# Gated integers of 30 of 48 units finished inside the up stage of a quantised feed-forward block

## What is computed

```
h    = act_qdq(layernorm(x))
up   = act_qdq(h @ Wup.T);  gate = act_qdq(h @ Wgate.T)
sig  = fixed_qdq_u16(sigmoid(gate))
gate = act_qdq(gate * sig)
o    = act_qdq(gate * up)
out  = x + o @ Wdown.T
```

## Time and profile before

| | |
|---|---|
| median of 3 runs | 2597.03 us (2592.02 to 2599.91) |
| profiled execution | 2596.16 us, its span 2594.1 us |
| gate, up and down stage, PE's matmuls | 751.6 to 1250.7, 1269.0 to 1769.0, 2087.6 to 2587.8 us |
| product stage | 1777.4 to 2062 us |
| PE, DVE, ACT busy over the span | 78%, 75%, 59% |
| DMA | 633.62 MB, mean 244 GB/s |

### The profile page before, as it was taken

The page is one execution under the profiler, slowest core; times in us unless marked ns, Lnnn a source line. Parts: engine busy times, 40 slices in busy tenths (PEclk is TensorE's granted clock), DMA queues, the critical chain, the costliest instruction groups (busy, mean ns, idle before and its releaser), DMA issues. The chain is left out here.

```text
span 2594.1 us, 26958 instructions
## 1 busy us (share of the span) xinstructions
PE 2023.5 (78%) x9560; PEld 948.2 (37%) x9560; DVE 1948.7 (75%) x1548; ACT 1518.1 (59%) x1507; POOL 420.4 (16%) x342
## 2 busy tenths in 40 slices
PE   4278888888659999999799999992000089999999
PEld 1134444444324444444344444441000034444444
DVE  8689999999824434532488888887999899877782
ACT  2536666666532322322466666666999898777770
POOL 0257676676600000000000000000000000000000
PEclk9589999999979999999899999996555589999999
DMA  7588888888344855732488888886777565555551
GB/s 267 208 366 322 331 317 331 323 314 332 126 162 163 245 195 176 248 130 114 187 285 287 290 287 286 290 278 270 277 274 275 197 239 211 218 221 228 228 204 65
DMA packets 142136, 633.62 MB, mean 244 GB/s; under 512 B 11616, under 2 KB 12128, under 8 KB 101856
## 3 DMA queue, kind: packets, MB, share of 16 engines
q1 hardware_dynamic: 132080, 495.61, 53.7%
q0 software_dynamic: 9216, 134.22, 13.4%
q10 hardware_dynamic: 752, 2.62, 0.3%
HBM read 453.23 MB, written 179.18 MB: 244 GB/s over the span
## 5 line engine op out<-in xcount | busy, mean ns | idle before, releaser
L1421 PE MATMUL fo_py<-kept_down,kept_gate 128*128 128x512 f16 x1536 | 459.0, 381 | 318.6 <-DVE kept_up L1402 318.6
L1182 PE MATMUL up_pp<-up_ah,kept_up 128*128 128x512 f16 x1536 | 459.0, 380 | 18.0 <-DVE up_al L1110 18.0
L1033 PE MATMUL ga_pp<-ga_ah,kept_gate 128*128 128x512 f16 x1536 | 458.3, 380 | 18.0 <-DVE ga_al L939 18.0
L1421 PEld LDWEIGHTS fo_py<-kept_down,kept_gate 128*128 128x128 f16 x1536 | 150.7, 98 | 501.5 <-DVE kept_up L1402 319.1
L979 DVE TENSOR_REDUCE kept_gate_peak<-ga_raw 128x1 f32<-128x2048 f32 x48 | 109.7, 2286 | 296.9 <-ACT ga_raw L1019 296.9
L1421 PE MATMUL fo_py<-kept_down,kept_up 128*128 128x512 f16 x768 | 292.1, 380 | 0.0
L1182 PE MATMUL up_pp<-up_al,kept_up 128*128 128x512 f16 x768 | 292.1, 380 | 0.0
L1033 PE MATMUL ga_pp<-ga_al,kept_gate 128*128 128x512 f16 x768 | 291.8, 380 | 0.0
L1019 ACT ACTIVATE ga_raw<-ga_pp 128x1024 f32<-128x1024 f32 x96 | 98.0, 1023 | 316.3 <-PE ga_pp L1033 316.3
L687 POOL TENSOR_TENSOR at_kv_rows<-at_kv_rows 128x1024 f32<-128x1024 f32 x64 | 215.0, 3360 | 158.0 <-DVE at_kv_rows L623 156.9
L1182 PEld LDWEIGHTS up_pp<-up_ah,kept_up 128*128 128x128 f16 x1536 | 150.7, 98 | 201.0 <-DVE up_al L1110 18.5
(11 more groups left out here) (194 smaller groups left out, 3565.2 us busy)
## 6 DMA issues: line engine op xcount, KB each, us to landing
gate_scratch<-ga_raw SPq DMA_DIRECT2D x48, 1024.0 KB, 4.9
up_gin<-gate_scratch SPq DMA_DIRECT2D x48, 1024.0 KB, 9.2
up_scratch<-up_raw SPq DMA_DIRECT2D x48, 1024.0 KB, 4.9
pp_ui<-up_scratch SPq DMA_DIRECT2D x48, 1024.0 KB, 5.6
fo_ui<-up_scratch SPq DMA_DIRECT2D x48, 1024.0 KB, 9.2
gate_integers<-up_gq SPq DMA_DIRECT2D x48, 512.0 KB, 9.7
pp_gq<-gate_integers SPq DMA_DIRECT2D x48, 512.0 KB, 3.6
fo_gi<-gate_integers SPq DMA_DIRECT2D x48, 512.0 KB, 7.3
```

Of the source, the lines that this page charges most:

```text
L1033: mm = nc.tensor.matmul(pp[k % 4][:, h, :], wt[w][:, c, f:f + P], a[:, b % 2, :, c, :], start=(q == 0), stop=(q == len(todo) - 1))
L1182: mm = nc.tensor.matmul(bank[:, h, :], wt[w][:, c, f:f + P], a[:, u % 2, :, c, :], start=(q == 0), stop=(q == len(todo) - 1))
L1421: mm = nc.tensor.matmul(py[(u * SUB + t) % 8][:, :], a[u % 2][:, f, t * P:(t + 1) * P], wt[w][:, f, :], start=(q == 0 and i == 0), stop=(q ...
```

## The change

- **h in integers.** The gate stage stores the integers of h (hq_d, 512 KiB a block), with two buffers for them; the up stage loads these and rounds nothing.
- **First pass, packed.** In the up stage three gate units go with every two up units (first_units), so that all 48 are through after 32 of 48 up units. Every third rounding of the gate is ACT's, the others are DVE's. ACT makes |gate| as integers (ab), and one DVE instruction multiplies it with the integer sigmoid and takes the maximum. The gate integers of the last 9 units (KEPT) stay in SBUF; 39 go to DRAM.
- **Second pass.** In the last 15 up units (from SECOND = 33) the gated integers of 30 units (READY), two per up unit, are made: the 9 kept ones, then units 0 to 20, loaded again. Each is a sigmoid (ACT), its scaling and one scalar_tensor_tensor (DVE), and is stored over the gate integers in gate_q.
- **Product stage.** The last three raw up units stay in SBUF. 30 units need only an absolute value, 17 of them on ACT, 13 on DVE (times -1, then maximum); 18 "late" ones go the old way. The order is a fixed list, 3 late ones in 8, with deeper rings (6 gate integers, 5 up units, 6 absolute values). The scales are made in the up stage.
- **Down stage.** For the 30 units the loaded integers are multiplied as they are; the 18 late ones (21 to 38) go the old way.
- All four stages are written out; pipeline, Tick and Transfers are gone.

```diff
+READY = 30
+KEPT = 9
...
@@ feed_gate
-        hq = s.sb("hq", [P, DC * BLK], I16)
+        hq = s.sb("hq", [P, 2, DC * BLK], I16)
...
+                def store_h(b):
+                    sp.wait_ge(m["hq"], b + 1)
+                    sp.dma_start(hq_d[b], hq[:, b % 2, :]).then_inc(hq_out[b % 2], 16)
...
@@ feed_up
+    AWAY = NU - KEPT
+    SECOND = NU - READY // 2
...
+    def first_units(n):
+
+        return [u for u in range(NU) if 2 * (u // 3) + (u % 3 == 2) == n]
+
+    def second_units(n):
+
+        return [v for v in range(READY) if SECOND + v // 2 == n]
...
+                load_h(0)
+                for u in range(GR):
+                    load_gate(u)
+                for n in range(NU):
+                    if n % UNITS == 0:
+                        load_h(n // UNITS + 1)
+                    for u in first_units(n):
+                        load_gate(u + GR)
+                        store_gate(u)
+                    if n == SECOND:
+                        for w in range(QR - 1):
+                            load_again(w)
+                    if n >= 1:
+                        store_raw(n - 1)
+                    for v in second_units(n - 1):
+                        store_gated(v)
+                    for v in [v for v in second_units(n - 1) if v >= KEPT]:
+                        load_again(v - KEPT + QR - 1)
...
+                def sigmoid_integer(k):
+                    dve.wait_ge(m["sig"], k + 1)
+                    sq_free(dve, k)
+                    nc.vector.tensor_scalar(sq[:, :], sig[:, k % 2, :], 65536.0, 65535.0, ALU.mult, ALU.min).then_inc(m["sq"], 1)
+
+                def first(u):
+                    sigmoid_integer(u)
+                    gate_integers(u + 2)
+                    dve.wait_ge(m["ab"], u + 1)
+                    dve.wait_ge(m["sq"], u + 1)
+                    nc.vector.tensor_tensor_reduce(out=sig[:, u % 2, :], in0=ab[:, u % 2, :], in1=sq[:, :], scale=1.0,
+                                                   scalar=0.0, op0=ALU.mult, op1=ALU.max,
+                                                   accum_out=keep["gated_peak"][:, u:u + 1]).then_inc(m["gpeak"], 1)
+
+                def second(v):
+                    sigmoid_integer(NU + v)
+                    dve.wait_ge(m["sq"], NU + v + 1)
+                    nc.vector.scalar_tensor_tensor(out=again(v), in0=sq[:, :], scalar=g[:, 7:8], in1=again(v),
+                                                   op0=ALU.mult, op1=ALU.mult).then_inc(m["g2"], 1)
...
+                for n in range(NU):
+                    if n % UNITS == 1 and n // UNITS + 1 < NB:
+                        split(n // UNITS + 1)
+                    for u in first_units(n):
+                        first(u)
...
+                    for v in second_units(n)[:1]:
+                        second(v)
+                    up_peak(n)
+                    for v in second_units(n)[1:]:
+                        second(v)
...
+                def first(u):
+                    act.wait_ge(gate_in[u % GR], 16 * (u // GR + 1))
+                    if u % 3 == 0:
+                        gq_free(act, u)
+                        nc.scalar.activation(integers(u), gin[:, u % GR, :], ACT.Copy, scale=g[:, 5:6]).then_inc(m["gq_act"], 1)
+                    need(act, m["gpeak"], u - 1)
+                    nc.scalar.activation(ab[:, u % 2, :], gin[:, u % GR, :], ACT.Abs, scale=g[:, 5:6]).then_inc(m["ab"], 1)
+                    have_gq(act, u)
+                    nc.scalar.activation(sig[:, u % 2, :], integers(u), ACT.Sigmoid, scale=g[:, 4:5]).then_inc(m["sig"], 1)
...
+                for n in range(NU):
+                    for u in first_units(n)[:1]:
+                        first(u)
+                    for v in second_units(n)[:1]:
+                        second(v)
+                    evict(n, 0)
+                    for u in first_units(n)[1:]:
+                        first(u)
+                    for v in second_units(n)[1:]:
+                        second(v)
+                    evict(n, 1)
...
@@ product_peak
+    GR, UR, AR, AHEAD = 6, 5, 6, 4
+    ready = [n for n in range(N - UNITS, N)] + list(range(N - KEPT, N - UNITS)) + list(range(READY - KEPT))
+    waiting = list(range(READY - KEPT, N - KEPT))
...
+                        nc.vector.tensor_scalar(neg[:, :], slot(gq, k), -1.0, None, ALU.mult).then_inc(m["neg"], 1)
...
+                        nc.vector.tensor_tensor(slot(ga, k), slot(gq, k), neg[:, :], ALU.max).then_inc(m["ga_dve"], 1)
...
@@ feed_out
+    GR, UR = 4, 3
+    FIRST = READY - KEPT
...
+    def late(n):
+        return FIRST <= n < NU - KEPT
```

## The result

The changed kernel takes **2550.43 us** (median of 4 runs, 2549.47 to 2551.67) against 2596.98: ratio 0.9821, 95% interval 0.9807 to 0.9835. It is faster by 46.5 us; 82 were forecast, and 2550.4 lies above the stated range of 2501 to 2547. The profiled execution has a span of 2547.6 us.

A forecast was written before the change was run, and what follows sets the result against it. Matmuls bound the up and down stages, VectorE and ScalarE the product stage. Seams -3.7, +2.3 and -4.4 and product stage -76.6 sum to -82.4 us: 2596.2 becomes 2514 us, range 2501 to 2547.

The forecast's parts named there:

- What bounds the kernel: Up and down stages: 500 us of unbroken matmuls each; product stage: VectorE and ScalarE full, so work moved under matmuls saves time.
- Up stage, first 32 slots: First pass, per two slots of 20.82 us: VectorE 18.8 us (90%), ScalarE 18.1 us (87%); evictions may lag 15.6 us.
- Up stage, last 15 slots: Second pass, two units a slot: VectorE needs 30.0 of 31.2 us per three slots, fits narrowly; nothing charged.
- the signs that the prediction named for being wrong: Up stage: TensorE waits for evictions or ScalarE for gate loads; product stage: products start over 4.3 us apart on average.
- Transfers: Up stage, first 32 slots: 344 GB/s needed against 340 at full share; 3 us of lag, nothing charged.
- The transfer rival: Up stage held by transfers: at 300 GB/s the first 32 slots lose 33 us, total 2547 us; chance 0.16.
- Seams: Between stages: gate to up gains 3.7 us, up to product loses 2.3, product to down gains 4.4.
- Product stage: VectorE and ScalarE 190 us each; stage taken as 208 us against 284.6, gain 76.6 us.
- the upper end: Product stage with both engines in step at every unit: 217 us, 226 with the head; lower end 199.
- in step: Rival, product stage: engines go unit by unit, or held by loads, 226 us instead of 208, total 2532; chance 0.11.
- the handshake: Rival, up stage's first pass: ScalarE and VectorE take turns, 11.6 us a unit against 6.94, total 2722 us; chance 0.05.

The follow-up runs named there:

- the deep ring: Changed kernel with second-pass reloads put into the gate loads' four free buffers, seven units ahead instead of three: 2514.58 us, ratio 0.9682.
- 32 units: Changed kernel with reloads seven units ahead in the gate loads' buffers, and 32 units instead of 30 finished in the up stage: 2512.62 us, ratio 0.9674.

## Why the prediction was wrong, point by point

- **What bounds the kernel** was right: work moved beneath the matmuls was hidden as long as it had no wait of its own.
- **Up stage, first 32 slots**: right. 90% and 87% were forecast for VectorE and ScalarE, 87% and 82% came, and no lag that TensorE felt.
- **Up stage, last 15 slots: this step failed.** It said "Three slots: ... 30.0 of 31.2 us. It fits, narrowly". As a sum for VectorE that holds: scalar_tensor_tensor took 2.35 us (2.32 taken), and with the deep ring VectorE is at 95% and the pace is TensorE's. But it was a sum, where for the first pass I had followed the order of instructions from engine to engine. In the second pass I followed neither SyncE's queue nor the reload. The reload is issued behind a store that waits for the up peak and behind another that waits for the rounding, three units ahead in a ring of four: a loop of 14 us in a slot of 10.41. Of the signs that the prediction named for being wrong, two are there: TensorE waits for evictions, and ScalarE for loads of gate integers. The step cost 35.3 us; with the loop opened in two different ways the kernel takes 2513.6 and 2514.6 us, and 2514 was forecast.
- **Transfers**: not short, as forecast. The 344 GB/s were reached only where loads and stores are densest, at a share of 0.93 and not 1.01; over the first pass it was 323 GB/s. The transfer rival got near the measured time (2547) with a mechanism that isn't there: the first 32 slots lost nothing. What I had not listed is a wait for one transfer that is issued late, behind others.
- **Seams**: -3.8, +3.1, -5.5 for -3.7, +2.3, -4.4. The order of loads that decides the last one was named, and moving it gave its 2.5 us.
- **Product stage**: 209.6 us for 208. VectorE starts 8.1 us behind the first load (9.0 taken), is busy for 193.8 us (190 taken) and idle for 7.8. For this idle time I had taken 9, a third of the way to the upper end, and no row stood behind that third: that it fits so well is luck. The prices hold in their rows, the cast's 0.69 for the negation among them:

```profile
L1181 DVE SCALAR_TENSOR_TENSOR up_gq<-up_sq,kept_g,up_gq 128x2048 int16<-128x2048 uint16 x21 | 49.4, 2351 | 0.7
...
L1383 DVE TENSOR_TENSOR kept_gate<-kept_up,pp_neg 128x2048 int16<-128x2048 int16 x13 | 15.9, 1226 | 0.5
...
L1380 DVE TENSOR_SCALAR pp_neg<-kept_up 128x2048 int16<-128x2048 int16 x13 | 8.9, 686 | 0.0
```

- **The rivals**: the stage did not run in step (209.6, not 226), and the handshake held.

## What to carry to other kernels

A stage that fits by busy time still has to be followed once around every loop of waits, SyncE's queue included: what is the load behind, what does that store wait for, and does the turn close within the slot. Where a ring is reloaded, put the load ahead of stores that wait for late work, or deepen the ring from buffers that are idle by then. When a wait is cheapened and nothing moves, look at what the transfer behind it now has around it in the queue.

## What the runs showed of the hardware

- **When a load lands depends on the transfers around it in SyncE's queue.** From issue a reload of 0.5 MiB took 4.8 us in the changed kernel, where the raw store had landed and two gated stores had 1.3 and 2.9 us to go. It took 6.6 us with the raw store and one gated store issued less than a microsecond before, 6.8 us with the raw store and both gated stores under way, and 5.7 us with one gated store in front and the second reload and the raw store right behind. How these transfers share the DMA engines isn't shown.
- **Loads alone run faster than the product stage's row of before suggested.** I had taken 359 GB/s as that stage's rate at full share. With the deep ring it moved 381, with 32 units 385 GB/s over 150 us, which is what the down stage's row of before pointed to (385). The Trainium skill (DMA: Bandwidth & Descriptors, Where 436 GB/s comes from) puts the limit between HBM and SBUF at about 358 GB/s for a core, half of what one stack of HBM gives its two cores. On this one core, with the others idle, that isn't a ceiling, and the measurement decides. What two cores of a stack get together no run here shows.
- **Waits of TensorE of some 3 us cost its clock as well.** In the changed kernel its matmuls took 14.2 us longer from first to last than before: it waited for 9.0 us, and it was busy for 505.2 us instead of 500.0. The matmuls right behind the waits of 3.09 and 3.43 us took 0.61 to 0.63 us instead of 0.38. Behind those of 0.80 and 1.00 us they took 0.38 to 0.39, and the clock stayed at 1.00 (1740 to 1750 us). One wait in TensorE's timeline, and the stretches; the granted clock of 0.64 is a mixture of 2.4 and 1.2 GHz:

```profile
1760.64 0.61 PE L1264 MATMUL up_pp<-up_ah,kept_up 128*128 128x512 f16 x1 [3.43 <-ACT kept_up_raw L1219]
...
1265.80:1780.00 514.20, 505.17 (x2304) 226.70 (x2304) 424.68 (x309) 353.60 (x233) 0.35 (x1) 0.98 0.78 288
...
1740.00:1750.00 10.00, 8.67 (x40) 3.82 (x41) 7.30 (x5) 5.71 (x4) 0.00 (x0) 1.00 0.45 159
...
1762.00:1768.00 6.00, 6.00 (x20) 2.28 (x19) 5.82 (x5) 1.39 (x2) 0.00 (x0) 0.64 0.72 293
```

Where evictions are late enough, this comes on top of the wait.
